# Layer 3 of a four-layer convolution: one engine copies the sums out and issues the stores and the next sample's loads, pair by pair

## The reference

```
x = x + _L0_conv_ref(_gn(x), L0_conv_w1, L0_conv_b1, L0_conv_w2, L0_conv_b2)
x = x + _L1_conv_ref(_gn(x), L1_conv_W)
x = x + _L2_conv_ref(_gn(x), L2_conv_w1, L2_conv_b1, L2_conv_w2, L2_conv_b2)
x = x + _L3_conv_ref(_gn(x), L3_conv_w1, L3_conv_b1, L3_conv_w2, L3_conv_b2)
```

## Time and profile before

| | before |
|---|---|
| median of 3 runs | 4344.64 us (4337.99 to 4358.8) |
| the profiled execution, its own time | 4354.15 us |
| its span, first to last instruction | 4352.3 us |
| TensorE busy | 3142.5 us, 72% of the span |
| VectorE, ScalarE, GpSimd busy | 2069.2, 1786.4, 1957.0 us |
| mean granted TensorE clock | 0.873 |
| moved by DMA | 829.46 MB, mean 191 GB/s |

### The profile page before, as it was taken

The page is one execution under the profiler, slowest core; times in us unless marked ns, Lnnn a source line. Parts: engine busy times, 40 slices in busy tenths (PEclk is TensorE's granted clock), DMA queues, the critical chain, the costliest instruction groups (busy, mean ns, idle before and its releaser), DMA issues.

```text
span 4352.3 us, 69714 instructions
## 1 busy us (share of the span) xinstructions
PE 3142.5 (72%) x26176; PEld 2008.6 (46%) x26176; DVE 2069.2 (48%) x6038; ACT 1786.4 (41%) x2626; POOL 1957.0 (45%) x3175
## 2 busy tenths in 40 slices
PE   0675987758876588865887667867778759777598
PEld 0443645435454354633545434554445535445355
DVE  2626643266432764327543275333844257432573
ACT  2433633335333463434534354333543436324232
POOL 1326544264432653336533464425643265431754
PEclk9987998879988798987998879888889889888799
DMA  6288697876969769596694967969678697786946
GB/s 210 57 147 168 151 318 200 155 164 140 340 175 170 159 159 322 159 195 153 182 330 119 212 148 197 306 118 216 149 217 292 109 212 165 234 270 111 200 76 218
DMA packets 589270, 829.46 MB, mean 191 GB/s; under 512 B 489731, under 2 KB 490502, under 8 KB 572550
## 3 DMA queue, kind: packets, MB, share of 16 engines
q1 hardware_dynamic: 323200, 734.28, 66.5%
q10 hardware_dynamic: 216582, 76.68, 8.2%
q0 software_dynamic: 49152, 14.05, 2.0%
HBM read 375.89 MB, written 267.45 MB: 148 GB/s over the span
## 4 chain that ended last, share of the span: by engine, by line
PE 46%; DMA 21%; DVE 9%; SPq 8%; ACT 5%; POOL 4%; ACTq 3%; issue 3%; DVEq 0%; POOLq 0%
PE acc L961 26%; PE acc L978 14%; SPq L327 6%; DMA dense_out<-arena 5%; DMA out<-y 4%; DMA arena<-x 4%; POOL y L510 4%; PE acc L1040 3%; DMA arena<-signs 3%; DVE dense_stats L860 2%; DMA signs<-arena 2%; DMA arena<-y 2%; ACT arena L599 2%; ACTq L535 2%; ACTq L606 2%
## 5 line engine op out<-in xcount | busy, mean ns | idle before, releaser
L961 PE MATMUL acc<-y,arena 64*128 64x384 f32 x9216 | 1749.3, 508 | 190.1 <-ACT y L568 129.0
L961 PEld LDWEIGHTS acc<-y,arena 64*128 64x128 f32 x9216 | 1013.6, 197 | 777.4 <-ACT y L568 229.2
L327 POOL DMA_DIRECT2D arena<-y x1536 | 790.6, 522 | 837.3 <-PE acc L978 736.4
L568 ACT ACTIVATE y<-acc 128x768 f32<-128x768 f32 x832 | 645.1, 807 | 1177.5 <-PE acc L978 1176.6
L978 PE MATMUL acc<-arena 64*128 64x384 f32 x4608 | 953.9, 509 | 195.2 <-issue 195.2
L489 POOL TENSOR_SCALAR arena<-arena,cst,fill 128x24 f32<-128x24 f32 (+1 forms) x1536 | 614.3, 419 | 701.8 <-issue 450.4
L510 POOL TENSOR_TENSOR y<-arena,y 128x3072 f32<-128x3072 f16 x88 | 529.8, 6043 | 734.5 <-DMA arena<-dense_out 734.3
L860 DVE BATCH_NORM_STATS2 dense_stats<-y 128x6 f32<-128x192 f32 x1536 | 408.0, 345 | 728.4 <-POOL y L510 728.2
L978 PEld LDWEIGHTS acc<-arena 64*128 64x128 f32 x4608 | 518.1, 196 | 422.3 <-issue 228.2
L1040 PE MATMUL acc<-arena,wd_side 128*32 128x384 fp8e4 (+1 forms) x10752 | 470.4, 329 | 290.3 <-DMA arena<-signs 231.5
L802 DVE TENSOR_SCALAR_CACHE_REDUCE y<-acc 128x768 f32<-128x768 f32 x256 | 245.1, 958 | 624.3 <-PE acc L978 624.3
(11 more groups left out here) (84 smaller groups left out, 1145.6 us busy)
## 6 DMA issues: line engine op xcount, KB each, us to landing
y<-x SPq DMA_DIRECT2D x64, 2304.0 KB, 26.1
out<-y SPq DMA_DIRECT2D x64, 2304.0 KB, 23.6
arena<-y SPq DMA_DIRECT2D x768, 141.0 KB
arena<-x SPq DMA_DIRECT2D x168, 576.0 KB, 6.4
dense_out<-arena ACTq DMA_DIRECT2D x384, 192.0 KB, 6.9
arena<-dense_out SPq DMA_DIRECT2D x192, 384.0 KB, 6.8
arena<-y SPq DMA_DIRECT2D x768, 71.9 KB
arena<-signs SPq DMA_DIRECT2D x192, 250.0 KB, 10.4
```

The lines of the kernel that those rows point to most:

```text
L327: eng.dma_start(halo[at:at + n, slot, :, d0:d0 + size], y[source:source + (n - 1) * step + 1:step, first + odd:first + odd + 3:2, s0:s0 + ...
L568: nc.scalar.activation(y[:, 2 * g:2 * g + 2, k * KN:(k + 1) * KN], acc[:, 2 * k:2 * k + 2, 0:KN], ACT.Identity, accum_out=sums[:, g, k:k + ...
L961: nc.tensor.matmul(acc[:, 2 * k + odd, 0:KN], w_center[at, slot, 2 * q + odd, :], y[at, 2 * g + odd, k * KN:(k + 1) * KN], start=turn == 0 ...
```

## The change

In layer 3 all three thirds of each pair are copied out by ScalarE (`evictor`). ScalarE also issues the store of the pair behind its copies, and the next sample's loads: those of pairs 0 and 1 three pairs behind their stores, the others seven pairs behind, so that the last seven are issued in layer 0 of the next sample. A store or load is one pair (2 channels) instead of a batch (4). SyncE issues no store, and no load but sample 0's.

Now 28 channels are loaded ahead, in three buffers; the third is VectorE's buffer `dense_stats`, free in layers 2 and 3. 16 have their sums on ScalarE in layer 2, each one pair later than before (`g - 1` behind pair `g`; the last one behind pair 0 of layer 3). 4 have their statistics on VectorE in layer 2, 8 on VectorE in layer 3, one behind each of the first 8 pairs. The 4 that arrive in `y` follow at pairs 10 and 11.

```diff
+AHEAD_FIRST = 4
+AHEAD_ACT = [(AHEAD_FIRST + i, i % 2) for i in range(PAIRS)]
+AHEAD_WITH = [2, 6, 10, 13]
+AHEAD_DVE = [(AHEAD_FIRST + PAIRS + n, 2) for n in range(len(AHEAD_WITH))]
+AHEAD_LATE = [(AHEAD_FIRST + PAIRS + len(AHEAD_WITH) + n, (0, 2, 1)[n % 3]) for n in range(8)]
+AHEAD_SLOTS = 3
+ARRIVE_WITH = 10
+LOAD_WITH = [g + (3 if 2 * g < AHEAD_FIRST else 7) for g in range(PAIRS)]
...
-    if d % ND == 0:
-        return "act" if k == 1 else "dve"
-    return "dve" if d % ND == 2 and k == 0 and g < AHEAD_LATE else "act"
+    return "dve" if d % ND == 0 and k != 1 else "act"
...
+        def load_next(eng, s, g):
+
+            eng.wait_ge(stored[g], 16 * (s + 1))
+            load(eng, s + 1, g)
...
                 for b in range(BATCHES):
-                    load_ahead(s, 2 * b + AHEAD_SLOTS)
                     halos(first + b + HALO_SLOTS)
-                    load_ahead(s, 2 * b + AHEAD_SLOTS + 1)
+                    for i in (2 * b + 1, 2 * b + 2):
+                        if 2 <= i < PAIRS:
+                            load_ahead(s, AHEAD_ACT[i])
+                    if b in (1, 3, 5):
+                        load_ahead(s, AHEAD_DVE[b // 2 + 1])
+                    if b == BATCHES - 1:
+                        load_ahead(s, AHEAD_LATE[1])
+                        load_ahead(s, AHEAD_LATE[0])
...
                     evict(d, g)
+                    if s > 0 and PAIRS + g in LOAD_WITH:
+                        load_next(act, s - 1, LOAD_WITH.index(PAIRS + g))
                     if g > 0:
                         pair_signs(s, g - 1)
...
                     evict(d + 1, g)
-                    if s < B - 1:
-                        ahead_stats(s, g)
+                    if s < B - 1 and g > 0:
+                        ahead_stats(s, g - 1)
                 root(d + 2)
                 for g in range(PAIRS):
                     evict(d + 2, g)
+                    store(act, s, g)
                     if s < B - 1:
-                        if g < AHEAD_LATE:
-                            ahead_stats(s, PAIRS + g)
+                        if g in LOAD_WITH:
+                            load_next(act, s, LOAD_WITH.index(g))
+                        if g == 0:
+                            ahead_stats(s, PAIRS - 1)
```

More of the change, by code:

```diff
@@ L245, in conv_preact_kernel @@
         w_halo = w_all[:, W_CHUNKS * BATCH_CH * P:].rearrange("p (k q m) -> p k q m", k=W_CHUNKS, q=BATCH_PAIRS)
-        ahead = part(A_STAGE, AHEAD_SLOTS * N * 4, F32).rearrange("p (k n) -> p k n", k=AHEAD_SLOTS)
+        ahead = [part(A_STAGE + k * N * 4, N * 4, F32) for k in range(2)] + [dense_stats[:].rearrange("p c w s -> p (c w s)")]
         stage_bytes = part(A_STAGE, 2 * STAGE_BYTES, F8)
@@ L276, in conv_preact_kernel @@
         setup_done = sem("setup_done")
-        loaded = [sem(f"loaded{b}") for b in range(BATCHES)]
-        stored = [sem(f"stored{b}") for b in range(BATCHES)]
+        loaded = [sem(f"loaded{g}") for g in range(PAIRS)]
+        stored = [sem(f"stored{g}") for g in range(PAIRS)]
         ahead_in = [sem(f"ahead_in{k}") for k in range(AHEAD_SLOTS)]
@@ L335, in wait_evicted, with wait_ahead, load, store @@
                 eng.wait_ge(acc_free[k], pairs)
+        def wait_ahead(eng, s, entry):
+            slot = entry[1]
+            order = [e for e in AHEAD if e[1] == slot]
+            eng.wait_ge(ahead_in[slot], 16 * (s * len(order) + order.index(entry) + 1))
+        def load(eng, s, g):
+            at = slice(2 * g, 2 * g + 2)
+            eng.dma_start(y[:, at, :].rearrange("p c n -> p (c n)"),
+                          x[s, :, at].rearrange("p c g w -> p (c g w)")).then_inc(loaded[g], 16)
+        def store(eng, s, g):
+            wait_evicted(eng, (s * ND + ND - 1) * PAIRS + g + 1)
+            at = slice(2 * g, 2 * g + 2)
+            eng.dma_start(out[s, :, at].rearrange("p c g w -> p (c g w)"),
+                          y[:, at, :].rearrange("p c n -> p (c n)")).then_inc(stored[g], 16)
+        def load_next(eng, s, g):
+            eng.wait_ge(stored[g], 16 * (s + 1))
+            load(eng, s + 1, g)
         def wait_halo_source(eng, bt):
@@ L343, in wait_halo_source @@
             if li == 0:
-                eng.wait_ge(loaded[b], 16 * (s + 1))
+                for g in range(b * BATCH_PAIRS, (b + 1) * BATCH_PAIRS):
+                    eng.wait_ge(loaded[g], 16 * (s + 1))
             elif li == 1:
@@ L409, in load_dense @@
                                      src.rearrange("(i j) c n -> j i (c n)", j=S)).then_inc(d_loaded[n % D_SLOTS], 16)
-            for b in range(BATCHES):
-                load(0, b)
+            for g in range(PAIRS):
+                load(sp, 0, g)
             sp.wait_ge(cleared, 3)
@@ L618, in _ @@
             for n, c in enumerate(act_channels(0, 0)):
-                act.wait_ge(loaded[c // BATCH_CH], 16)
-                channel_stats(c, y[:, c, :], ahead[:, n % AHEAD_SLOTS, :])
+                act.wait_ge(loaded[c // 2], 16)
+                channel_stats(c, y[:, c, :], ahead[n % 2])
             root(0)
```

115 lines of the change are left out of this document (60 added, 55 removed).

## The result

The changed kernel takes 4505.93 us (median of 4 runs, 4503.36 to 4508.66), the one before in the same session 4345.62 us (4337.99 to 4358.8): a ratio of 1.0354, 95% interval 1.0325 to 1.0383. The forecast was 4225 us, range 4080 to 4365.

A forecast was written before the change was run, and what follows sets the result against it. SyncE's queue order and DMA traffic were taken to bound the crossing between samples, the change removing only the order. From 4344.6 us, 252 less at crossings, 134 more in layer 2 and 2 less at the end gave 4225, range 4080 to 4365.

The forecast's parts named there:

- The sum: Whole kernel, from the median 4344.6 us: crossings 252 us less, layer 2 134 more, last store 2 less, giving 4225.
- the crossing: Layer 3 of one sample, the gap, layer 0 of the next; seven times; forecast 218 us instead of 253.5.
- layer 3's "about 100 us": Layer 3 before another sample: 93.5 us undisturbed plus 6 for VectorE's late loads and ScalarE held at its last issues.
- the chain that gave layer 0 its 113: Layer 0 after layer 3: 94 us plus a 19 us stall for signs, behind pair 9's load and batch 4's halos.
- Layer 2: Layer 2: a load 6.2 us late behind halos stalls three rounds by 6.4 us, 19 a sample, 134 in all.
- The rule that I set beside it: Layer 3: DMA engines alternate between loaded queues, so halos escape the stores; in one line, layer 3 stays at 118 us.
- The landing of pair 9: Layer 0's load of pair 9 lands 140 us after layer 3's first edge: 41.4 MB at 310 GB/s.
- the 9 us for the signs to land: Layer 0: the second sign DMA lands after 9 us, the wait ending near 160 us after layer 3's first edge.
- The traffic rival: Traffic is the bound, not order: 270 GB/s, pair 9's load 20 us later, crossing 237 us, 4364 us; chance 0.12.
- The held ScalarE: ScalarE is held at its DMA issues by a full queue, its copies too: crossing 245 us, 4418 us; chance 0.13.
- The passage: From layer 3 to the next sample's layer 0: 5 us instead of 10.
- The ends: Last store half as large, 2 us less; moving the zeroing and using `dense_stats` as a buffer cost nothing.

The follow-up runs named there:

- the three orders with the lag of four: Changed kernel with layer 2's sum loads, layer 3's late loads and layer 0's signs issued before halos, loads four pairs behind stores: 4259.35 us, 0.9782.

## Why the prediction was wrong, point by point

**The sum.** From the median of before I forecast 120 us less, and 161 us more came. Most of the difference is the crossing: 218 us forecast, 253.9 measured, 35.9 us too few, seven times, 251 us. Of the 35.9, layer 3 has 14.6 (114.6 for 100), the gap 0.9, layer 0 20.4 (133.4 for 113). So two steps failed, layer 3's "about 100 us" and the chain that gave layer 0 its 113.

**What bounds the kernel.** I named two bounds, the order of one queue and the traffic, and then let the change take away nearly all that the order was said to cost. Here they act together: in SyncE's queue the order decides which small transfer stands behind which, and the traffic decides how long that is. Turning round the late loads or the signs alone moved the stall on by a pair or two; halving the bytes shortened the crossing by 38 us with every order as it was.

**Layer 2** was right, in place, cause and size: stalls of 6.6 us for 6.4, at three rounds of a sample (in two of the seven samples spread over four), 20.7 us for 19, 145 us for 134. Putting the load ahead of the halos took it away.

**Layer 3 is the first step that failed.** "It prepares weights a pair or more ahead, so a load that is some us late doesn't reach TensorE. I give layer 3 93.5 + 6 = about 100 us, ..." It took 114.6. I had sized "some us" by layer 2's loads; in layer 3 VectorE waited 20.96 and 16.91 us, more than its lead of a pair or two. Even a nearly empty load kept it waiting 19.77 us, and with no late loads at all layer 3 was 105.0 us, because the halos are late themselves. For these my sum had no price in layer 3: I knew a set of eight from layer 2, 7.44 us to issue, and beside full stores in another queue it took 11.7 to 15.4 us in the last layer 3 of the changed kernel.

**The rule that I set beside it.** By the Trainium skill (DMA: Bandwidth & Descriptors, Queues, rings and completion order) the DMA engines take turns between queues. From that I concluded that halos gain by not standing behind stores. The runs don't contradict the turns, but they contradict the conclusion. In the last layer 3, where no loads go, the halos fare worse beside the stores (14.0 us a set and 99.6 us in the changed kernel) than in one queue with them (11.5 at most, 89.3).

**Layer 0 is the second, by two terms of its chain.** The landing of pair 9 was forecast 140 us after the first edge and came at 159 to 168. Until then 45.9 to 46.4 MB had been moved, where I had counted 41.4, and at 277 to 291 GB/s, where I took 310. Full windows did run at 304 to 359 GB/s, but the transfers don't stay full: layer 3's own stalls leave them at 0.49. The lag of seven pairs also holds back loads whose stores have long landed; with a lag of four and the orders mended pair 9 landed at 141 to 145. And the 9 us for the signs to land were 22.8 to 26.5. So the wait for signs ended 191 to 199 us after the edge, not near 160; in the kernel before it had ended at 194 to 200.

**"A longer layer 3 would hardly change this sum, since the landing sets the end; ..."** That fell too, and the trace of before could have told it: the same load landed at 134 to 141 us there, and the crossing took 254.5. The kernel whose loads landed at the forecast moment had a crossing of 240.5 us, not 218: layer 3 117.1 instead of 100, layer 0 118.4 instead of 113.

**Rivals.** The traffic rival (4364) came nearest in its cause, and it had the landing right, 20 us later than mine; its price, 16 us of gain per crossing left, was still too kind. The held ScalarE (4418) had the sign right and, in the changed kernel, the mechanism wrong: it was SyncE that was held, while a store cost ScalarE 0.34 us to issue. **The passage** took 5.9 us for 5. **The ends**: I counted 2 us gained at the last store; the last layer 3 lost 6 (93.3 to 102.0 us in the traces with its stores in ScalarE's queue), because I had not asked what stores in a second queue do to halos where nothing else changes.

What stays open: why the crossing stays at 238.5 us or more with all of its bytes in every one of these kernels. From pair 9 on layer 0 runs at its own 6.1 us a pair in all of them, so what is lost is lost before that. Late loads are worth 11.5 us of it and the pairs' bytes 37.6; the lag and the issuing engine trade layer 3 against layer 0. Also open is why giving the stores back to SyncE shortened layer 0 and not layer 3, and why single loads and sign DMAs behind others need up to 35 us to land. Spreading the late loads over layer 2 was not tried. The fastest versions that move all the bytes are the three orders with the lag of four, 0.9782, and the same with the last stores in twos, 0.9761, or from SyncE, 0.9799; their intervals overlap.

## What to carry over

When a change gives a consumer its data a step earlier, look at where each load stands in its queue: here a shift by one pair behind eight small transfers cost 134 us. Where a sum ends on one event, look up when that event came in the trace of before: the landing that I forecast as a gain lay there already. A transfer that is moved to another engine's queue to relieve the first still shares the DMA engines with it, so price the small transfers that stay behind by a stretch in which both run, and if there is none, let the range say so. And where TensorE's stall holds back the stores, the stall empties the DMA engines as well, so the bytes can't be divided by the rate of a full stretch.

## What the hardware showed that I had not expected

- In the last layer 3, issuing eight halos took SyncE 11.8 to 16.1 us with full stores in ScalarE's queue, 8.4 to 10.2 with half the bytes in these, 7.2 to 11.5 with the stores in its own queue; in a quiet layer 2 it took 7.3.
- A load of 24 KB behind such halos needed as long as 19 us to land; one of 576 KB in the same place up to 30.6.
- Five such loads of 576 KB, issued by ScalarE ahead of its stores instead, took up to 35.1 us.
- The second of two sign DMAs issued together took 22.8 to 26.5 us to land in the changed kernel, the first 5.2 to 9.6.
